# Edge stage of a graph-transformer layer: tile numbers in registers, later softmax links, one-hot blocks on ScalarE

## The reference

```python
e = el[src] + er[dst]
e = jnp.where(e >= 0, e, NEG_SLOPE * e)
e_max = jax.ops.segment_max(e, dst, num_segments=N)
exp_e = jnp.exp(e - e_max[dst])
denom = jax.ops.segment_sum(exp_e, dst, num_segments=N)
a = exp_e / jnp.maximum(denom[dst], 1e-16)
msg = feat_v[src] * a[:, :, None]
rst = jax.ops.segment_sum(msg, dst, num_segments=N)
...
x = x + gnn(xn, src, dst) + mix(xn)
x = x + ffn(layernorm(x))
```

## Time and profile before

| | us |
|---|---|
| median of three runs | 3512.27 |
| lowest and highest | 3508.56, 3518.39 |
| the profiled execution | 3480.26 |
| its span, first to last instruction | 3478.4 |
| edge steps, first to last (L1566) | 834.6 to 2430.8 |

### The profile page before, as it was taken

One profiled execution on the slowest core, in us unless ns is written; L12 is line 12 of the kernel. 1 busy time (PEld: TensorE's weight loads), 2 busy tenths in 40 slices (PEclk: granted clock), 3 DMA queues, 4 the chain that ended last, 5 costly groups with the idle time before them and its releaser, 6 DMA issues. The chain is left out here.

```text
span 3478.4 us, 50828 instructions
## 1 busy us (share of the span) xinstructions
PE 2417.5 (69%) x11245; PEld 1803.3 (52%) x11246; DVE 1829.6 (53%) x3903; ACT 909.8 (26%) x1917; POOL 1338.1 (38%) x1406
## 2 busy tenths in 40 slices
PE   3899998666777877777877777777233329999500
PEld 3677776223555555555555555555233328888400
DVE  5544443786666655566556655565353334444433
ACT  0111111011333333333333333333443313333100
POOL 0000000302565555565556555652144342222244
PEclk8899998898888878888788878889555559999755
DMA  3122222644555555655656556653655634444576
GB/s 115 49 68 68 68 68 77 228 167 134 165 162 159 157 164 163 169 160 154 169 164 171 166 154 173 170 163 89 221 134 136 131 76 134 145 145 145 168 257 232
DMA packets 238264, 507.89 MB, mean 146 GB/s; under 512 B 50320, under 2 KB 76432, under 8 KB 238208
## 3 DMA queue, kind: packets, MB, share of 16 engines
q0 software_dynamic: 85936, 274.85, 28.6%
q1 hardware_dynamic: 134752, 196.94, 18.5%
q10 hardware_dynamic: 17520, 35.44, 3.0%
HBM read 394.73 MB, written 112.37 MB: 146 GB/s over the span
## 5 line engine op out<-in xcount | busy, mean ns | idle before, releaser
L618 POOL DMA_INDIRECT arena<-v_table,idx x832 | 917.2, 1102 | 847.1 <-PE ps L1566 670.1
L1566 PE MATMUL ps<-arena 128*128 128x260 f32 x3328 | 975.4, 441 | 315.9 <-issue 289.6
L1566 PEld LDWEIGHTS ps<-arena 128*128 128x128 f32 x3328 | 678.5, 216 | 533.2 <-issue 427.7
L757 ACT ACTIVATE arena<-ps x832 | 501.9, 603 | 1096.2 <-PE ps L1566 668.4
L1182 DVE TENSOR_TENSOR arena<-arena 128x512 f32<-128x512 f32 x832 | 547.1, 683 | 0.0
L1384 PE MATMUL ps<-arena 128*128 (+4 forms) x1994 | 423.8, 336 | 94.3 <-DMA arena<-q_table 73.8
L1389 PE MATMUL ps<-ident,arena 128*128 128x128 f32 x1128 | 213.8, 308 | 328.1 <-DVE arena L1257 257.2
L1384 PEld LDWEIGHTS ps<-arena 128*128 128x128 f32 (+1 forms) x1994 | 275.7, 195 | 224.8 <-issue 115.3
L1389 PEld LDWEIGHTS ps<-ident,arena 128*128 128x128 f32 x1128 | 151.0, 159 | 349.3 <-DVE arena L1257 262.2
L658 POOL DMA_INDIRECT arena<-xn_table,e_idx x105 | 99.3, 945 | 281.5 <-PE ps L1389 265.0
L595 POOL TENSOR_SCALAR ag<-ag 128x1 f32<-128x1 f32 x49 | 10.7, 219 | 502.3 <-DVE ag L999 502.2
(11 more groups left out here) (282 smaller groups left out, 3470.0 us busy)
## 6 DMA issues: line engine op xcount, KB each, us to landing
y_table<-arena SPq DMA_DIRECT2D x105, 256.0 KB, 2.5
arena<-local_table ACTq DMA_DIRECT2D x52, 512.0 KB, 4.2
arena<-in_x SPq DMA_DIRECT2D x98, 256.0 KB, 2.7
arena<-v_table,idx POOLq DMA_INDIRECT x832
v_table<-arena SPq DMA_DIRECT2D x49, 260.0 KB, 2.9
agg<-arena SPq DMA_DIRECT2D x49, 260.0 KB
arena<-agg SPq DMA_DIRECT2D x49, 260.0 KB, 4.6
x_mix<-arena SPq DMA_DIRECT2D x49, 256.0 KB, 2.7
```

What stands on the lines that cost most here:

```text
L618: pool.indirect_dma_start(vg[:, j % 2 * U + i, :], None, v_table, bass.IndirectOffsetOnAxis(ap=idx[:, j, i:i + 1], axis=0))\
L757: act.activation(halves(fin[:, bass.ds(dst_, DH)], HALF), halves(ps[:, bass.ds(src_, 2 * D)], D)[:, :, 0:HALF], ACT.Copy).then_inc(s("act_ ...
L1566: last = pe.matmul(ps[:, bass.ds(acc + h * D, HALF)], hot[:, i // V % 2, i % V, :], vg[:, b * U + i, h * HALF:(h + 1) * HALF], start=False ...
```

## The change

- Tables: DVE works out two numbers for each chunk, the tile of its first step (`first_tab`) and a 16-bit word whose bit i says whether step i ends a tile (`turn_tab`), and the table of the tiles' ends. The tables by step are gone.
- Registers: PE, ACT and DVE load the two numbers of a chunk, and work out tile and turn of each step by shift, mask and addition (`turn_of`, `room_of`, `next_tile`). ACT also works out source, target and both counts of each copy. Its copies no longer wait for `step_mm`, and their wait for a store is one tile looser.
- The one-hot blocks go to ACT (`found`): four `Abs` of 128x128 with a bias from `dst_local`, then one `Relu` of 128x512 over one minus that. There are four groups instead of two, and PE waits for a new count, `hot_made`.
- The links of chunk c+1 come some steps later on DVE and PE, `factor` behind ACT's copy 10 and `weights` behind copy 12.

```diff
+def turn_of(eng, bits, i):
+
+    return eng.snap((bits >> i) & 1, min_val=0, max_val=1)
+
+
+def room_of(eng, d):
+
+    return eng.snap((d & 1) * (2 * D), min_val=0, max_val=2 * D)
+
+
+def next_tile(eng, d, turn):
+
+    return eng.snap((d + turn).with_bounds(min_val=0, max_val=NT - 1))
...
-        hot = at(o, 2, V, P); o += 2 * V * P
+        hot = at(o, U // V, V, P); o += U * P
...
+        def chunk_places(engine, c, n):
+
+            return list(zip(looked_up(engine, first_tab, c, n, NT - 1), looked_up(engine, turn_tab, c, n, 2 ** U - 1)))
...
-            def snapshots(t, n):
-                places = looked_up(ENGINE.Activation, act_tab, t * 2, 2 * n, DUMMY * D)
-                counts = looked_up(ENGINE.Activation, act_tab, t * 2 + 2 * ST, 2 * n, 32768)
-                for i in range(n):
-                    (src_, dst_), (closed, stored) = places[2 * i:2 * i + 2], counts[2 * i:2 * i + 2]
-                    act.wait_ge(s("step_mm"), t + (i + 1))
-                    if later(t, 1) or i:
-                        act.wait_ge(s("act_step"), t + i)
-                    act.wait_ge(s("tile_sum"), closed)
-                    act.wait_ge(s("fin_st"), stored)
-                    act.activation(halves(fin[:, bass.ds(dst_, DH)], HALF), halves(ps[:, bass.ds(src_, 2 * D)], D)[:, :, 0:HALF],
-                                   ACT.Copy).then_inc(s("act_step"), 1)
-
-            def chunk(c, b, r):
+            def snapshot(t, d, turn):
+                src_ = act.snap(DUMMY * D - (DUMMY * D - (d & 1) * (2 * D)) * turn, min_val=0, max_val=DUMMY * D)
+                dst_ = act.snap(4 * DH - (4 * DH - (d & 3) * DH) * turn, min_val=0, max_val=4 * DH)
+                closed = act.snap(d + turn + 1, min_val=1, max_val=NT + 1)
+                stored = act.snap(d * 16 + past("fin_st", -16 * 3)[1], min_val=16, max_val=32768)
+                if later(t, 1):
+                    act.wait_ge(s("act_step"), t)
+                act.wait_ge(s("tile_sum"), closed)
+                act.wait_ge(s("fin_st"), stored)
+                act.activation(halves(fin[:, bass.ds(dst_, DH)], HALF), halves(ps[:, bass.ds(src_, 2 * D)], D)[:, :, 0:HALF],
+                               ACT.Copy).then_inc(s("act_step"), 1)
+
+            def found(g, k):
+                if later(g, U // V):
+                    act.wait_ge(s("step_mm"), g * V + (V - U))
+                for i in range(V):
+                    last = act.activation(hot[:, k, i, :], col_no[:], ACT.Abs, bias=dst_local[:, bass.ds(g * V + i, 1)], scale=-1.0)
+                last.then_inc(s("hot_far"), 1)
+                apart(act, s("hot_far"), g + 1)
+                act.activation(hot[:, k], hot[:, k], ACT.Relu, bias=1.0, scale=-1.0).then_inc(s("hot_made"), 1)
+
+            def chunk(c, b, r, own):
...
+                for i in range(U):
+                    if i % V == 0 and (more or i < U - 2 * V):
+                        found(c * (U // V) + i // V + 2, (i // V + 2) % (U // V))
+                    last = not more and i == U - 1
+                    turn = 1 if last else turn_of(act, bits, i)
+                    snapshot(c * U + i, d, turn)
+                    if not last:
+                        d = next_tile(act, d, turn)
+                    if not more:
+                        continue
+                    if i == 10:
+                        factor(c + 1)
+                    elif i == 12:
+                        weights(c + 1, 1 - b)
...
-            def step(t, i, b):
-                if i % V == 0:
-                    wait_past(dve, s("step_mm"), t, V + 1)
-                    dve.tensor_tensor(hot[:, i // V % 2], col_no[:].unsqueeze(1).broadcast_to([P, V, P]),
-                                      dst_local[:, bass.ds(t, V)].unsqueeze(2).broadcast_to([P, V, P]), ALU.is_equal)
...
-                    if i == 2:
+                    if i == 5:
                         scored(c + 1, n, q)
-                    elif i == 4:
+                    elif i == 7:
                         run_max(c + 1, n)
-                    elif i == 6:
+                    elif i == 9:
                         linked(c + 1)
-                    elif i == 9:
+                    elif i == 11:
                         joined_max(c + 1, n)
-                    elif i == 12:
+                    elif i == 13:
...
-                for i, d in enumerate(tiles):
+                for i in range(U):
                     last = product(prep[:, i * 3 * H:(i + 1) * 3 * H],
-                                   [(hot_t[:, i * P:(i + 1) * P], er_flat[:, bass.ds(d * 3 * H, 3 * H)])])
+                                   [(hot_t[:, i * P:(i + 1) * P], er_flat[:, bass.ds(d * (3 * H), 3 * H)])])
+                    if i < U - 1:
+                        d = next_tile(pe, d, turn_of(pe, bits, i))
...
-                    marks[:] = looked_up(ENGINE.PE, pe_tab, t * 2, 2 * V + 1, 2 * D)
-                acc, turn, other = marks[i % V * 2:i % V * 2 + 3]
+                    pe.wait_ge(s("hot_made"), hot_group + 1)
...
+                    turn = turn_of(pe, bits, i)
+                    step(c * U + i, i, b, d, turn, c * (U // V) + i // V)
+                    d = next_tile(pe, d, turn)
                     if not more:
                         continue
-                    if i == 1:
+                    if i == 5:
                         turned_e(c + 1)
-                    elif i == 3:
+                    elif i == 7:
                         gathered_ends(c + 1)
-                    elif i == 5:
+                    elif i == 9:
                         spread_ends(c + 1)
-                    elif i == 8:
+                    elif i == 11:
+                        factors(c + 1)
+                    elif i == 12:
                         turned_max(c + 1)
```

155 lines of the change are left out of this document (63 added, 92 removed).

## The result

The changed kernel takes 4255.5 us, the median of four runs (4242.2 to 4267.6); the kernel before took 3514.8 (3508.6 to 3518.4). The ratio is 1.211, with an interval of 1.207 to 1.215: slower by 741 us, where 259 were forecast. The direction and the engine that the forecast named are right, the size is not: 4255 lies far outside 3620 to 3885. The profiled execution has a span of 4239.9 us.

The account below looks back on a forecast made before the run. PE led the chunk of 30.85 us; ACT was to become the bound at 35.5. The edge stage came to 1876 us against 1604, +272, less 13 for the tables: 3512 + 259 = 3771 us, range 3620 to 3885.

Parts of the forecast that it names:

- What decides: ACT's copies: register work behind the wait makes each 1.8 us instead of 0.79, 28.8 us a chunk for sixteen.
- The price of a register instruction: ACT's register work per copy: plain ones and moves 65 ns, fused ones 85 ns, together 1.16 us.
- ACT's end of a pass: ACT's loop branch: fetching a body of 688 instructions costs 1.5 us a pass, bounds nothing to 3 us.
- ACT never waits: ACT's chunk in the edge stage: its work summed to 35.5 us with no term for waits on other engines.
- The links: Later softmax links between DVE, PE and ACT: they cost at most 0.6 us a chunk.
- The links alone change nothing: Rival for the edge stage: the later links leave the time to one of the other cases; no chance of its own.
- PE: PE's chunk with register work for loads: 27 us warm, 31 with today's cold share, hidden under ACT's 35.5.
- The cheap-register rival: ACT's copies stay at 0.79 us, ACT needs 19 us, PE decides: 3299 us, or 3522 partly cold; chance 0.14.
- The cold loop: Rival: idle time keeps twelve PE steps at 1.2 GHz, PE needs 37 to 40 us a chunk, 3931 us; chance 0.12.
- The tables: Setup on DVE ahead of the first projection: 18.7 us of table work falls to 5.5, saving 13 us.
- the clean rows: ACT's copies and one-hot groups in a chunk: 28.8 and 5.2 us, 34.0 together.

Follow-up runs that it names:

- after_third: The changed kernel itself, run again unaltered in a later group of runs that showed no long register instructions: 3914 us, 1.119 of the kernel before.
- b_links: The kernel before with only the softmax links moved to the changed kernel's later steps: 3764 us, 1.076 of the kernel before.
- a_old: The changed kernel with the softmax links back at the old steps: 4074 us, 1.155 of the kernel before; the changed kernel in that group took 4211 us.
- a_tab_dve_old: The changed kernel with ACT's places from tables, one-hot blocks on DVE and links at old steps: 3420 us, 0.977 of the kernel before; in another group 3704 us, 1.050.
- a_tab: The changed kernel with ACT's copies reading places and counts from tables again, one-hot blocks still on ACT: 3772 us, 1.070 of the kernel before.
- b_hot: The kernel before with only the one-hot blocks moved to ACT, all tables and links as before: 3718 us, 1.062 of the kernel before.

## Why the prediction was right and wrong, step by step

**What decides: right.** ACT became the bound through register work behind its own wait. A clean copy follows at 1.76 to 1.77 us (predicted 1.8), of it 1.16 us without work (1.2). A copy with a group takes 3.10 us, so a group adds 1.33 (1.3); 16 x 1.77 + 4 x 1.33 = 33.6 us a chunk, forecast 34.0. The budget of the Trainium skill, ScalarE: Activation LUTs, Rules for kernel authors, would have priced the four `Abs` at 1.64 us. For one alone it is near (0.41 us, measured 0.39), but four in a row start 0.29 us apart and take 1.28, so here the row decided rightly.

**The price of a register instruction: the step that failed most, 334 of the stage's 498 us (770 less 272).** The prediction priced register instructions by their medians in the earlier trace rows. In the groups that show the long ones, they and the gaps beside them add 334 us to the stage (2374 less 2040); what causes them stays open. No row of the kernel before shows one, so its trace could not have given them; but the range took the bounds of each price to be within 10%, and a kind of work that grows from some 2300 to 9700 instructions on ACT deserved a wider end. It is not the only step that failed: by the ratio without long instructions, 1.119, the time would be 3932 us on this base, still above 3885. The next three paragraphs have the rest.

**ACT's end of a pass: right in kind, undersized.** The forecast had 1.5 us for the fetch of a body of 688, bounds 0 and 3, and three packets a pass. In after_third it is this:

```profile
1743.15 0.60 ACT L773 ACTIVATE arena<-ps  x1 [1.16 <-issue]
1747.99 0.36 ACTq L751 DMA_DIRECT2D arena<-local_table  x1
1748.52 0.60 ACTq L753 DMA_DIRECT2D arena<-pen_table  x1
1749.37 1.28 ACT L780 ACTIVATE arena<-col_no,arena 128x128 f32<-128x128 f32 x4 [5.62 <-issue]
```

From the branch to the next instruction pass 3.0 us (median), the upper bound, and there are eight packets a pass. With loads and issues a pass costs 7.1 us beside its copies and groups, 3.5 a chunk; forecast were 1.5 and 0.75, so 1.3 us a chunk or 65 us in all were missing. (By its own terms the prediction's high bound is 3952, not 3939: 24 x (2 x 38.3 + 3) + 77 + 70 = 2057 is 453 above 1604, less 13 is 440. The range doesn't rest on it.)

**ACT never waits: wrong.** The sum let ACT run without a wait. Its rows in after_third, 900 to 2400 us:

```profile
L773 ACT ACTIVATE arena<-ps x609 | 367.3, 603 | 678.8 <-issue 595.3 <-PE ps L1556 54.1 <-DMA agg<-arena 29.4
L762 ACT ACTIVATE arena<-arena 128x128 f32<-128x128 f32 x38 | 11.8, 309 | 27.6 <-DVE arena L1172 27.6
```

In 38 chunks it waits 54.1 us for PE's closing at the turns, 29.4 for stores and 27.6 ahead of the exponential: 2.9 us a chunk. Of the 39.4 us measured a chunk, 33.6 and 3.5 are told above, and 2.3 are left for these waits. For the stage that is some 120 us; it is what remains and not a reading of its own. An engine at its bound still hands over at each turn, and the other side is not always ready.

**The links: wrong.** The step that failed is "the later links cost at most 0.6 us a chunk". It took 2.0 us of DVE's scans and a step of PE from the factor on, and forgot what comes ahead of the factor: copy 10 and, at a turn, PE. Alone the links cost 5 us a chunk (b_links). In the changed kernel ACT's pace hides a part, as I read a_old; some of the rest shows in the waits above. "The links alone change nothing" was wrong outright.

**PE: right, in another kernel.** Expansions were to take 5.2 us, and take 5.2 us in a_tab_dve_old (1714.43 to 1719.66); a hot step 1.05, there 1.0. Its 29.5 us a chunk lie between the 27 of a warm PE and the 31 with today's cold share; the 2.75 us at the end of its pass hold two loads of 1.0 us, for which the sum had 0.9 a chunk. The cheap-register rival named this correctly as PE's time if ACT were free.

**The cold loop: did not come about as a bound.** PE's clock fell to 0.71 with its idle time, but in after_third it is 0.75 and ACT still leads.

**The tables: right in size, wrong in worth.** 15.8 us earlier at the first projection (forecast 13), but the edge stage starts at 827 us against 835: about half of it is lost on the way, and no run shows where.

Together: forecast +272 for the stage; less 19 for the clean rows, and 65 for the end of a pass, 120 for ACT's waits and 334 for the long instructions give +772; measured +770. That they meet says little, since the 120 is what the others left over.

## To carry to other kernels

Ask of register work on which side of the engine's own wait it stands and how many instructions the expression makes: half the instructions, or the same ones ahead of the wait, each gave back about half of this change's loss in the groups without long instructions. Ask the same of a load from a table: its price goes by how many numbers it brings, and 14 us of loads in a chunk of 31 left ACT no room for 5 us of new work. A link that passes through three engines is priced from the queue in front of it, not from itself: what stands ahead of the factor made 266 us of a move that looked free. And of a gain of 2% measured in one group of runs, ask for a second group: here 0.977 became 1.050 with the same program, so none of these versions is to be preferred to the kernel before.

## What the runs showed of the hardware

- Register instructions of 0.03 to 0.06 us can take 0.4 to 0.72 us, in bursts, on ACT's and PE's sequencers, in some groups of runs and not in others (0 or 244 of some 10,000 in one and the same program). All 2703 that were counted stand within 0.5 us of a packet of the gathers' queue, and none was left without the indirect transfers (one run). They come without instruction packets in the loop too (94 in a_tab), so the length of the loop is not their cause.
- A load of 2, 4, 6 or 8 numbers from an on-chip table into registers took 0.47, 0.89, 1.30 and 1.72 us on ACT, some 0.21 us for each number (kernel before, b_hot).
- ACT's loop stayed resident with bodies of 166 to 262 instructions (no packets, 0.22 us from branch to next instruction) and not with 318 (b_hot: five packets a pass, 2.5 us) or 338 to 856 (medians of 2.5 to 3.3 us). The Trainium skill, Runtime: NRT & Kernel Launch, Instruction fetch mechanics, gives most engines room for 512; in these runs the limit lies between 262 and 318. Where in the program a body begins, no run varied.
- An expression of constants minus products costs a move for each constant: the same value written as products plus constants took 9 register instructions in place of 17.
